# Layer 0's second attention adds its output bias on GpSimd; layer 2's state-space stage takes its weights from two PSUM banks and forms VectorE's sums behind one state

## The reference

```
y = x + o @ Wo + bo
```

```
h[t] = exp(delta[t] * a[n]) * h[t-1] + u[t] * B[t, n]
y[t] = sum over n of C[t, n] * h[t, n] + D * x[t]
```

## Time and profile before

| | |
|---|---|
| median of 3 runs | 4894.12 us (4886.29 to 4910.12) |
| the profiled execution | 4918.48 us, its span 4916.6 us |
| busy, of the span | PE 72%, PEld 47%, DVE 65%, ACT 48%, POOL 43% |
| layer 0's second attention, pipeline | 560 to 704 us of the span |
| layer 2's state-space stage | 2504 to 3165 us; its 8 groups of states 2567 to 3163 us |

### The profile page before, as it was taken

The page is one execution under the profiler, slowest core; times in us unless marked ns, Lnnn a source line. Parts: engine busy times, 40 slices in busy tenths (PEclk is TensorE's granted clock), DMA queues, the critical chain, the costliest instruction groups (busy, mean ns, idle before and its releaser), DMA issues. The chain is left out here.

```text
span 4916.6 us, 71516 instructions
## 1 busy us (share of the span) xinstructions
PE 3563.9 (72%) x20958; PEld 2316.4 (47%) x20958; DVE 3208.6 (65%) x6355; ACT 2374.5 (48%) x4470; POOL 2124.6 (43%) x2029
## 2 busy tenths in 40 slices
PE   6867566768884548885448888759974878677686
PEld 4657346723332423333322222336653658655586
DVE  5430662079997267884349999877867766666665
ACT  3334434455551337774235555437753645544345
POOL 0046005649992435553328888711222116401264
PEclk9978677979997779997669889859985879988798
DMA  2011101145551223320233334300000001100112
GB/s 87 21 33 42 44 21 34 44 105 91 93 93 27 83 78 90 90 61 10 62 97 68 69 70 72 55 20 1 1 3 3 0 31 39 65 10 0 34 39 79
DMA packets 223544, 241.37 MB, mean 49 GB/s; under 512 B 38845, under 2 KB 170660, under 8 KB 221460
## 3 DMA queue, kind: packets, MB, share of 16 engines
q1 hardware_dynamic: 200980, 192.20, 16.8%
q0 software_dynamic: 22272, 45.66, 3.0%
HBM read 174.13 MB, written 62.72 MB: 48 GB/s over the span
## 5 line engine op out<-in xcount | busy, mean ns | idle before, releaser
L2463 PE MATMUL s_l_attn_a_y_ps<-XN,c_ident 128*128 128x512 f32 x1024 | 572.4, 670 | 95.0 <-POOL XN L2481 78.1
L2533 DVE TENSOR_TENSOR_SCAN s_l_attn_a_h<-s_l_attn_a_da,XN 128x512 f32<-128x512 f32 x512 | 607.8, 1209 | 21.6 <-POOL XN L2489 14.9
L2471 ACT ACTIVATE s_l_attn_a_da<-s_l_attn_a_delta,s_l_attn_a_a 128x510 f32<-128x510 f32 x512 | 345.7, 685 | 398.0 <-DVE s_l_attn_a_h L2533 395.1
L1086 POOL DMA_INDIRECT XNT<-rows_x,s_l_ffn_ffn_from_row x284 | 278.6, 981 | 468.8 <-DVE s_l_ffn_ffn_to_row L948 383.4
L960 DVE COPY s_l_ffn_ffn_xt<-s_l_ffn_ffn_turned 128x128 f32<-128x128 f32 x284 | 79.7, 291 | 553.7 <-PE s_l_ffn_ffn_turned L1161 235.8
L1091 POOL DMA_INDIRECT rows_y<-PICK,s_l_ffn_ffn_to_row x284 | 298.1, 1050 | 291.2 <-ACT PICK L1032 231.5
L1172 PE MATMUL s_l_ffn_ffn_up<-s_l_ffn_ffn_xt,s_l_ffn_ffn_own_w 128*128 128x128 f32 x2272 | 337.2, 296 | 99.2 <-DVE s_l_ffn_ffn_xt L960 97.0
L2463 PEld LDWEIGHTS s_l_attn_a_y_ps<-XN,c_ident 128*128 128x128 f32 x1024 | 185.0, 203 | 421.3 <-POOL XN L2481 290.6
L4401 DVE TENSOR_REDUCE s_l_attn_b_top<-s_l_attn_b_m_ps 128x2 f32<-128x512 f32 x512 | 329.8, 687 | 81.7 <-PE s_l_attn_b_m_ps L4107 78.4
L1182 PE MATMUL s_l_ffn_ffn_down<-down,s_l_ffn_ffn_hid 128*128 x2272 | 326.8, 291 | 76.5 <-DVE s_l_ffn_ffn_hid L974 41.9
L2481 POOL TENSOR_TENSOR XN<-s_l_attn_a_h,LOG 128x512 f32<-128x512 f32 x256 | 326.5, 1290 | 78.1 <-DVE s_l_attn_a_h L2533 66.6
(11 more groups left out here) (721 smaller groups left out, 8480.6 us busy)
## 6 DMA issues: line engine op xcount, KB each, us to landing
LOG<-s_l_attn_a_c_kept SPq DMA_DIRECT2D x128, 256.0 KB, 4.1
s_l_attn_a_more_c_rows<-s_l_attn_a_c_kept SPq DMA_DIRECT2D x128, 256.0 KB, 4.1
...
```

Source lines behind the costliest of these rows:

```text
L1086: nc.gpsimd.indirect_dma_start(xin[j % RING], None, k.rows_x[:, :], bass.IndirectOffsetOnAxis(from_row[:, j:j + 1], 0)).then_inc(gathered[ ...
L2463: last = self.nc.tensor.matmul(self.y_ps[:, i, :], self.k.ident[:], self.hc[n % 2][:, i, :], start=(n == 0 and not begun), stop=(n == NST ...
L2471: self.nc.scalar.activation(self.da_half(g, n, i)[:, :, 1:], self.delta[par][:, i, :].rearrange("p (b t) -> p b t", b=BPG)[:, :, 1:], ACT. ...
L2533: self.nc.vector.tensor_tensor_scan(self.h[n % 2][:, i, :], self.da_half(g, n, i).rearrange("p b t -> p (b t)"), self.u[n % 2][:, i, :], 0 ...
```

## The change

In layer 0's second attention GpSimd adds the bias to X itself, one sequence at a time ahead of the powers of the same pair; the bias is loaded as 128 equal rows, the two bias matmuls of a pair go, and VectorE's `add_out` also waits for GpSimd's sum.

In layer 2's state-space stage TensorE spreads two weights, w in bank 0 and 1 - w in bank 1 of `aux` (the first token of a sequence takes w = 1, so 0 in bank 1). VectorE then makes `raw` and `ahead` from PSUM each, without the subtraction and the copy, and all five products and sums stand behind state 11. C no longer comes through TensorE (`move_c`) but by a DMA from the rows that SP has just stored. Several pieces stand behind other states than before.

```
 (l0_attn_b)
             with pool.Fori(0, PAIRS) as pair:
+                for m in range(2):
+                    x = k.X[:, bass.ds(pair * (2 * TPB) + m * TPB, TPB), :]
+                    nc.gpsimd.tensor_tensor(x, x, w["L0b_bo"][:].rearrange("p (t d) -> p t d", d=D), ALU.add).then_inc(bias_added, 1)
                 for m in range(2):
                     pool.wait_ge(var_ready, pair * 2 + (m + 1))
...
             def project_out(u, m):
                 pe.wait_ge(ont_ready, u + 1)
-                nc.tensor.matmul(o_ps[m], k.ones_row[0:1, 0:P], w["L0b_bo"][:], start=True, stop=False, skip_group_check=True)
...
             def add_out(u, m):
+                dve.wait_ge(bias_added, u + 1)
                 dve.wait_ge(y_ready, u + 1)
 (StateScan)
         sp.wait_ge(self.c_saved, 16 * (g + 1))
+        if low is not None:
+            rows, rows_landed = low
+            sp.dma_start(rows, self.c_kept[g % 2][NST:2 * NST, :]).then_inc(rows_landed, 16)
 (l2_attn_a, TensorE)
             def spread_lam(q):
                 pe.wait_ge(xp_ready, min(q + 2, GROUPS))
                 pe.wait_ge(lam_ready, q + 1)
-                nc.tensor.matmul(aux[:, 0, :], half_row[LAM:LAM + 2, :], lam[LAM:LAM + 2, :], start=True, stop=True).then_inc(lam_up, 1)
+                pe.wait_ge(cum_ready, q + 1)
+                pe.wait_ge(vt_ready, q + 1)
+                nc.tensor.matmul(aux[:, 0, :], half_row[LAM:LAM + 2, :], lam[LAM:LAM + 2, :], start=True, stop=True)
+                nc.tensor.matmul(aux[:, 1, :], rest_row[LAM:LAM + 2, :], lam[LAM:LAM + 2, :], start=True, stop=True).then_inc(lam_up, 1)
...
                 if q < GROUPS:
-                    if n == 5 and r < GROUPS:
+                    if n == 6 and r < GROUPS:
                         project_x(r)
-                    if n == 9:
+                    if n == 10:
                         spread_lam(q)
-                    if n == 10 and r < GROUPS:
+                    if n == 12 and r < GROUPS:
                         project_ssm(r)
-                    if n == 11:
+                    if n == 13:
                         project_z(q)
-                    if n == 14:
-                        if r < GROUPS:
-                            spread_mean(r)
-                        move_c(q)
+                    if n == 15 and r < GROUPS:
+                        spread_mean(r)
...
-                    if n == 12 and g + 2 < GROUPS:
+                    if n == 14 and g + 2 < GROUPS:
                         project_dt(g + 2)
 (l2_attn_a, GpSimd)
             def between(q, n):
+                if n == 8:
+                    turn_vt(q)
                 if n == 9:
-                    turn_vt(q)
-                if n == 10:
                     turn_bc(q)
 (l2_attn_a, ScalarE; sines no longer holds the Tanh, which is weigh)
                     if n == 7 and q < GROUPS:
+                        silu_table()
+                        weigh(q)
                         sines(q)
                         log_table()
-                    if n == 10:
+                    if n == 9:
...
-                        if n == 4:
+                        if n == 5:
                             keep_vt(q)
 (l2_attn_a, VectorE)
             def split_delta(q):
                 dve.wait_ge(lam_up, q + 1)
...
+                rest = aux[:, 1:2, :].rearrange("p a (b t) -> p a b t", b=BPG).to_broadcast([P, CHH, BPG, SEQ])
+                nc.vector.tensor_tensor(ahead[:, :, :, 0:SEQ - 1], delta[q % 2][:].rearrange("p i (b t) -> p i b t", b=BPG)[:, :, :, 1:SEQ],
+                                        rest[:, :, :, 1:SEQ], ALU.mult).then_inc(lam_read, 1)
...
-                nc.vector.tensor_tensor(cb, scan.rest[0:NST, :], aux[0:NST, 0, :], ALU.mult).then_inc(cb_ready, 1)
+                nc.vector.tensor_tensor(cb, cb, scan.rest[0:NST, :], ALU.mult).then_inc(cb_ready, 1)
...
-                        if n == (4 if g == 0 else 3):
+                        if n == 4:
                             sum_up_delta(q)
...
-                        if n == 10:
+                        if n == 11:
                             split_delta(q)
-                        if n == 11:
                             make_dx(q)
-                        if n == 15:
-                            multiply_cb(q)
```

More of the change, by code:

```diff
@@ L2947, in project_ssm @@
                 pe.wait_ge(xp_ready, q + 1)
+                since(pe, lam_read, q)
                 for i in range(CHH):
@@ L3170, in sizes @@
                 act.wait_ge(dt_up, q + 1)
-                since(act, dx_ready, q)
+                since(act, scan.dx_made, q)
                 since(act, delta_ready, q)
```

104 lines of the change are left out of this document (54 added, 50 removed).

## The result

The changed kernel takes 4865.15 us (median of 10 runs, 4851.62 to 4876.82), the kernel before beside it 4890.78 (10 runs, 4882.56 to 4910.12): ratio 0.9943, 95% interval 0.9929 to 0.9958, a gain of 25.6 us where the prediction had 11. The median gain, 0.57%, is just over the 0.5% at which the prediction drew its line for faster, and the interval (0.42% to 0.71%) has that line inside it.

A forecast was written before the change was run, and what follows sets the result against it. The prediction took TensorE's queue ahead of VectorE to bound layer 0's second attention, and VectorE to bound layer 2's state-space stage. Bias -14 and stage +3 gave -11 from 4894, so 4883 us, range 4850 to 4914.

The forecast's parts named there:

- rival 1: Whole kernel: the bias pays and the state-space stage comes out even; 4883 us, range 4868 to 4900, chance 0.55.
- rival 2: State-space stage gains too, contended instructions running free and no wait at state 8; -24 us, 4856, chance 0.22.
- The bias: Layer 0's second attention: dropping bias matmuls saves 2.0 us in six middle pairs, 1.8 behind the last; -14 in all.
- The tail's 1.8: Layer 0's second attention, behind the last pair: both bias matmuls lie on the path, removal saves 1.8 us.
- The stay: Layer 2: VectorE's two absences from its states, 11.0 us, become one of 8.1; -2.9 a group.
- GpSimd's turning: Layer 2, turnings moved a state earlier: VectorE newly waits for GpSimd's end product at state 11; +1.6 us a group.
- `keep_vt` with `count_turns`: Layer 2, ScalarE: `keep_vt` right behind `cum` and `count_turns` delays state 6's decay; +0.6 us a group.
- `multiply_cb`: Layer 2: moves from state 15, where VectorE waited anyway, to dense state 0; +0.7 us a group.
- TensorE, +0.4: Layer 2: projections moved to states 12 to 14, partly at half clock, lengthen the stretch; +0.4 us a group.
- rival 3: Layer 2: TensorE becomes the bound in states 12 to 15 through lasting half clock; 4935 us, chance 0.12.
- The stage, +3: Layer 2's state-space stage: terms sum to +0.4 us a group over seven groups, +3 in all.
- Rival 4: Layer 0's second attention: the bias brings nothing because something else is late instead; 4897 us, chance 0.07.

The follow-up runs named there:

- e3: Kernel before with layer 0's output bias left out and nothing adding it; 4685.93 us against 4700.54 for the kernel before.
- e12: Kernel before with layer 0's output bias matmul issued twice in a row; 4708.06 us against 4698.70 for the kernel before.
- e4: Changed kernel with `ahead` in its old form, a subtraction with two SBUF inputs and a drain; 4681.04 us against 4700.54 for the kernel before.
- e7: Changed kernel with ScalarE's `gate_z` moved behind state 7 and `keep_vt` behind state 6; 4680.45 us against 4702.09 for the kernel before.
- a1: The changed kernel itself, run again on another chip than the follow-up's first ones; 4678.68 us against 4702.09 for the kernel before.
- e2: Changed kernel with the bias put back on TensorE, only layer 2's edits left; 4698.59 us against 4700.54 for the kernel before.
- e1: Kernel before with only layer 0's output bias moved to GpSimd; 4685.99 us against 4700.54 for the kernel before.

## Why the prediction was right, and where it was not

- **As a whole.** 4865 lies in the range, 4850 to 4914, but so does no change at all (4891 to 4894), and it lies 3 below the range of rival 1 (4868 to 4900), between its 4883 and rival 2's 4856; the likeliest outcome named, same within 0.5% (0.61), is missed by the median. A gain of 25.6 where 11 was forecast is right in its direction and in the bias; that the number fell inside is in part the width of the range.
- **The bias, -14: mechanism right, size 16.9.** The wait for `st` fell to the 10 forecast, GpSimd's sums are hidden (e3), the seventh pair gave nothing. The term mis-sized is "2.0 for six middle pairs", which the traces put at 2.6. It was read off one pair, 638.3 to 657.4 (and its first matmul as 0.6 where the row has 0.69), which with 19.1 us was one of the two short ones; the other four took 20.0 to 20.4, and in the one shown under e12 both bias matmuls and all that follows up to `st` are at half clock. 16.9 is at the edge of the prediction's bounds, 9 to 17. Even the upper end of a pair, 2.4, counted only the bias matmuls' own time. The tail's 1.8 was too much: 0.8.
- **The stay, -2.9 (bounds -5.1 and -1.8): -3.8.** L3319 ran at 1.21, the three others in the group shown at 1.72, 1.74 and 1.35, between the held-up and the free case. Of this, e4 puts 0.7 to 1.1 on the second bank and the drain that it saves; what the copy and the gathering give, no run separates.
- **GpSimd's turning, +1.6: 0.33**, and not because GpSimd was early. The gating of x that I had put under this wait came first: ScalarE's 1.06 in state 10 held VectorE, and GpSimd caught up meanwhile (in e7, where that wait is moved away, those for GpSimd rise from 9.0 to 14.7). Together they are 1.4. `keep_vt` with `count_turns`, +0.6: 0.51. `multiply_cb`, +0.7: it takes 0.86 in its new place, +0.2 of work over before; whether its 0.65 lay under a wait there, as I assumed, no run separates. Not foreseen are a wait of 0.5 to 1.0 for the spread just ahead of the stay in five of the six groups, and one of 1.55 for the second bank in three groups of all (six in a1). The piece ahead of the stay was forecast at +2.9 and has +3.0 here, +4.0 in a1: right in sum by luck, with other waits than those named.
- **TensorE, +0.4: -0.3.** It idled 4.0 at the stay on average, as forecast. The half clock that rival 3 feared came in three of the six groups, and only for part of the four states: 0.62 over nine microseconds, then 1.00. Before, those nine microseconds were at 0.55 to 0.62 in all six.
- **The stage, +3: -8 in the two profiles.** e2 has -2 (-7 to +4), a1 less e1 -9, the pooled profiles -4: between nothing and -9. By the table two terms were mis-sized, the stay by 0.9 a group and TensorE by 0.7. But the base moves as much: I set the terms against group 1 and took the mean of the groups as given, while the mean held three groups of 77 to 79, of which the same code has two in e1, one in e3 and three in e12. I took 0.5%, 24 us, for what a measurement can tell; the interval here is 7 us to either side.
- **Rival 2** (stage gains 24) was wrong: the stay fell between its value and the forecast's (7.2 us, against 5.9 and 8.1), and waits took most of it back. **Rival 4** was wrong (e1). Of the 14.6 us between -11 and -25.6, 2.9 are the bias, about 7 the stage if the pooled -4 is taken, and the rest is open.
